# A recommendation model on one Trainium2 core: seven of 416 row gathers are fetched by SP, one row per DMA

## The reference

```python
x = dense_inputs                                   # 2048 x 13
for W, b, g, be in bot:                            # 13 -> 512 -> 256 -> 64
    x = _bn(relu(x @ W + b), g, be)
embs = tbl[idx] for each of 26 tables              # 2048 x 26 x 64, tables 12500 x 64
T = concatenate([embs, x[:, None, :]], axis=1)     # 2048 x 27 x 64
Z = einsum('bnd,bmd->bnm', T, T)
R = concatenate([x, Z[:, upper triangle]], axis=1)
h = R
for W, b, g, be in top:                            # 415 -> 512 -> 256 -> 1
    h = _bn(relu(h @ W + b), g, be)
return sigmoid(h)
```

## Time and profile before

| | |
|---|---|
| median of 3 runs | 581.65 us (581.29 to 582.29) |
| the profiled execution's own time | 581.63 us |
| its span, first to last instruction | 579.8 us |
| busy: PE / DVE / ACT / POOL | 373.9 / 239.1 / 189.4 / 395.8 us |
| gathers of POOL in the loop | 390, mean 946 ns |
| gathers of POOL in the last part | 26, mean 946 ns |
| mean granted clock of PE | 0.763 of full speed |

### The profile page before, as it was taken

How to read it: one execution, slowest core, us unless ns; L and a number is a source line. 1 busy time by engine, 2 the same in 40 slices (tenths; PEclk the granted TensorE clock), 3 DMA queues, 4 the chain that set the end, 5 groups by cost and what they waited for, 6 DMA issues and landing times.

```text
span 579.8 us, 13905 instructions
## 1 busy us (share of the span) xinstructions
PE 373.9 (64%) x5827; PEld 276.7 (48%) x5827; DVE 239.1 (41%) x646; ACT 189.4 (33%) x509; POOL 395.8 (68%) x426
## 2 busy tenths in 40 slices
PE   6959769668778182745638282735638292767995
PEld 2328437466476171533626162533526171556782
DVE  5772254644644242424323242524224142455532
ACT  4742135425325050413214041413214050454223
POOL 5777777777777777777777777777777777771100
PEclk9999787798798577575858566675958566688998
DMA  8222121221212121122122121212212121220000
GB/s 236 61 27 27 26 28 28 29 29 28 30 28 28 27 29 29 28 28 28 26 28 29 28 29 26 29 25 29 29 27 29 26 29 26 29 29 9 2 0 2
DMA packets 15896, 18.31 MB, mean 32 GB/s; under 512 B 7614, under 2 KB 8894, under 8 KB 15695
## 3 DMA queue, kind: packets, MB, share of 16 engines
q0 software_dynamic: 13312, 13.66, 17.7%
q1 hardware_dynamic: 2524, 3.72, 2.0%
HBM read 17.34 MB, written 0.01 MB: 30 GB/s over the span
## 4 chain that ended last, share of the span: by engine, by line
POOL 66%; issue 22%; PE 7%; ACT 1%; DVE 1%; DMA 1%; POOLq 0%; DVEq 0%; ACTq 0%
POOL emb L322 63%; POOL emb L333 3%; PE l_bank L395 3%; PE l_bank L509 1%; PE l_bank L401 1%; ACT Zs L282 1%; PE z_bank L353 1%; DMA emb<-table,stage 0%; PE l_bank L556 0%; DMA idx_raw<-idx 0%; PE l_bank L506 0%; PE tr_bank L481 0%; PE l_bank L518 0%; PE tr_bank L353 0%; ACT logit_sq L696 0%
## 5 line engine op out<-in xcount | busy, mean ns | idle before, releaser
L322 POOL DMA_INDIRECT emb<-table,stage x390 | 368.9, 946 | 121.7 <-issue 118.6
L282 ACT ACTIVATE Zs<-z_bank 27x112 f32<-27x112 f32 (+3 forms) x272 | 92.2, 339 | 210.2 <-PE z_bank L457 204.4
L443 PE MATMUL tr_bank<-ident,emb 128*128 128x128 f32 x195 | 39.5, 328 | 139.4 <-DMA emb<-table,stage 119.5
L256 DVE COPY Zs<-z_bank 27x112 f32<-27x112 f32 (+3 forms) x272 | 88.7, 326 | 48.2 <-PE z_bank L457 43.0
L471 PE MATMUL l_bank<-Zs,tw_sb 128*128 128x128 f32 x840 | 105.8, 279 | 0.0
L471 PEld LDWEIGHTS l_bank<-Zs,tw_sb 128*128 128x128 f32 x840 | 101.3, 196 | 0.0
L855 DVE COPY TT<-tr_bank 128x512 f32<-128x512 f32 (+1 forms) x60 | 55.4, 972 | 108.9 <-PE tr_bank L443 108.3
L443 PEld LDWEIGHTS tr_bank<-ident,emb 128*128 128x128 f32 x195 | 25.3, 160 | 152.2 <-issue 104.5
L457 PE MATMUL z_bank<-TT 64*27 64x26 f32 x3840 | 59.7, 217 | 31.7 <-issue 20.3
L457 PEld LDWEIGHTS z_bank<-TT 64*27 64x27 f32 x3840 | 53.6, 133 | 40.0 <-issue 37.7
L866 DVE BATCH_NORM_STATS2 stats_t<-h_part 128x128 f32 x60 | 17.7, 294 | 110.4 <-ACT hidden_hi L650 110.4
(11 more groups left out here) (124 smaller groups left out, 279.4 us busy)
## 6 DMA issues: line engine op xcount, KB each, us to landing
emb<-table,stage POOLq DMA_INDIRECT x416, 2.7
tw_sb<-tw0x SPq DMA_DIRECT2D x1, 1792.0 KB, 9.2
bw_sb<-bw SPq DMA_DIRECT2D x1, 512.0 KB, 3.7
tw_sb<-tw SPq DMA_DIRECT2D x1, 512.0 KB, 11.9
twx_sb<-twx SPq DMA_DIRECT2D x1, 256.0 KB, 10.0
idx_raw<-idx SPq DMA_DIRECT2D x1, 169.0 KB, 3.1
bw_sb<-bw SPq DMA_DIRECT2D x2, 64.0 KB, 3.8
hidden<-dense_t SPq DMA_DIRECT2D x1, 104.0 KB
```

The source lines that it names most:

```text
L256: last = copy(dst, src[:, :, ZC * q:ZC * q + w])
L282: return nc.scalar.activation(dst, src, ACT.Copy)
L322: pool.indirect_dma_start(out=emb[:, s, k, h, :], out_offset=None, in_=table, in_offset=bass.IndirectOffsetOnAxis(ap=stage[:, s, col:col + ...
L443: tr = nc.tensor.transpose(tr_bank[g % 2][:, c * P:(c + 1) * P], emb[:, s, k, :, :].rearrange("p h d -> p (h d)"), ident[:, :])
```

## The change

SP fetches seven gathers' rows, each row with a DMA of its own: 128 rows of 256 bytes each, 896 DMAs in all. Five of the seven are the gather of pair 12, h = 0, in the third part of each loop iteration (parts 2, 5, 8, 11 and 14, all in slot 2); their rows go straight to their place in `emb`. Two are the gathers of pairs 0 and 1, h = 0, of the last part; their rows go to a new buffer `emb_sp`, which has no other writer, so these rows need no open slot. POOL leaves the seven gathers out.

The row numbers come from a new input `sp_idx`, which SP loads and DVE turns into `sp_rows` with four small operations. SP reads 16 of them at a time into registers, and issues a DMA from each. Before the rows of a part it waits for the slot to be open. The table `SP_ORDER` puts the work in order. PE waits for a semaphore of SP's rows beside that of POOL's.

```diff
+SP_SLOT = SLOTS - 1
+SP_PAIR = TP - 1
+SP_LAST = 2
+SP_SETS = LOOPS + SP_LAST
+SP_BATCH = 16
+SP_ORDER = (("part", 0, 0, 128),
+            ("last", 0, 0, 96),
+            ("part", 1, 0, 128),
+            ("last", 0, 96, 128),
+            ("part", 2, 0, 128),
+            ("last", 1, 0, 64),
+            ("part", 3, 0, 128),
+            ("last", 1, 64, 128),
+            ("part", 4, 0, 128))
...
             sp.dma_start(dense_sb[:, :], dense_t).then_inc(bottom_loaded, 16)
+            sp.dma_start(sp_raw[:, :, :], sp_idx).then_inc(sp_idx_loaded, 16)
             sp.dma_start(bw0_sb[:, :], bw0).then_inc(bottom_loaded, 16)
...
+            regs = [sp.alloc_register("sp_row%d" % r) for r in range(SP_BATCH)]
+            sp.wait_ge(sp_rows_ready, 1)
+            for kind, n, p0, p1 in SP_ORDER:
+                if kind == "part":
+                    sp.wait_ge(slot_open, n * SLOTS + SP_SLOT + 1)
+                for at in range(p0, p1, SP_BATCH):
+                    row_set = n if kind == "part" else LOOPS + n
+                    sp.load(regs, sp_rows[row_set:row_set + 1, at:at + SP_BATCH])
+                    for p, reg in enumerate(regs, at):
+                        row = sp.snap(reg, min_val=0, max_val=NF * VOCAB - 1)
+                        if kind == "part":
+                            sp.dma_start(emb[p:p + 1, SP_SLOT, SP_PAIR, 0, :],
+                                         table[bass.ds(row, 1), :]).then_inc(landed_sp_part, 16)
+                        else:
+                            sp.dma_start(emb_sp[p:p + 1, n, :],
+                                         table[bass.ds(row, 1), :]).then_inc(landed_sp_last[n], 16)
...
                     for k in range(TP):
                         for h in range(2):
+                            if (s, k, h) == (SP_SLOT, SP_PAIR, 0):
+                                continue
...
                     for k in range(k0, k1):
+                        if h == 0 and k < SP_LAST:
+                            continue
...
-                        pe.wait_ge(landed[s][g], (it + 1) * (len(pairs) * 2 * 16))
+                        by_sp = 1 if s == SP_SLOT and SP_PAIR in pairs else 0
+                        pe.wait_ge(landed[s][g], (it + 1) * ((len(pairs) * 2 - by_sp) * 16))
+                        if by_sp:
+                            pe.wait_ge(landed_sp_part, (it + 1) * (P * 16))
...
-                pe.wait_ge(landed_last[h][g], (LAST_GROUPS[g][1] - LAST_GROUPS[g][0]) * 16)
+                k0, k1 = LAST_GROUPS[g]
+                by_sp = SP_LAST if (h, g) == (0, 0) else 0
+                pe.wait_ge(landed_last[h][g], (k1 - k0 - by_sp) * 16)
+                for k in range(by_sp):
+                    pe.wait_ge(landed_sp_last[k], P * 16)
...
+            dve.wait_ge(sp_idx_loaded, 16)
+            step = chain(sp_step, 0)
+            step(nc.vector.tensor_scalar(sp_neg[:, :], sp_raw[:, 0, :], 0.0, float(VOCAB), ALU.is_lt, ALU.mult))
+            step(nc.vector.tensor_tensor(sp_neg[:, :], sp_raw[:, 0, :], sp_neg[:, :], ALU.add))
+            step(nc.vector.tensor_scalar(sp_clamped[:, :], sp_neg[:, :], 0.0, float(VOCAB - 1), ALU.max, ALU.min))
+            nc.vector.tensor_tensor(sp_rows[:, :], sp_clamped[:, :], sp_raw[:, 1, :], ALU.add).then_inc(sp_rows_ready, 1)
             nc.vector.memset(idle_operand[:, :], 0.0).then_inc(consts_ready, 1)
```

More of the change, by code:

```diff
@@ L92, in quadrant_columns, with rec_program @@
     return min(ZC, NF - ZC * q)
-def rec_program(nc, idx, table, dense_t, params, identity, bw0, bw1, bw2, tw0x, twx, tw1, out):
+def rec_program(nc, idx, sp_idx, table, dense_t, params, identity, bw0, bw1, bw2, tw0x, twx, tw1, out):
     ctx = ExitStack()
@@ L114, in rec_program @@
         stage = sb("stage", [P, SLOTS, PW], U32)
+        sp_raw = sb("sp_raw", [SP_SETS, 2, P], I32)
+        sp_neg = sb("sp_neg", [SP_SETS, P])
+        sp_clamped = sb("sp_clamped", [SP_SETS, P])
+        sp_rows = sb("sp_rows", [SP_SETS, P], U32)
+        emb_sp = sb("emb_sp", [P, SP_LAST, D])
         emb = sb("emb", [P, SLOTS, TP, 2, D])
@@ L186, in rec_program @@
         landed = [[sem("landed%d_%d" % (s, g)) for g in range(GROUPS)] for s in range(SLOTS)]
+        sp_idx_loaded = sem("sp_idx_loaded")
+        sp_step = sem("sp_step")
+        sp_rows_ready = sem("sp_rows_ready")
+        landed_sp_part = sem("landed_sp_part")
+        landed_sp_last = [sem("landed_sp_last%d" % k) for k in range(SP_LAST)]
         landed_last = [[sem("landed_last%d_%d" % (h, g)) for g in range(len(LAST_GROUPS))] for h in range(2)]
@@ L476, in last_transposes @@
             def last_transposes(h, g):
-                pe.wait_ge(landed_last[h][g], (LAST_GROUPS[g][1] - LAST_GROUPS[g][0]) * 16)
+                k0, k1 = LAST_GROUPS[g]
[3 more added lines that the diff above has]
+                    pe.wait_ge(landed_sp_last[k], P * 16)
                 for c, (k, k_end) in enumerate(last_blocks(g)):
+                    source = emb_sp if h == 0 and k < SP_LAST else emb_last[:, h, :, :]
                     tr = nc.tensor.transpose(last_tr_bank[g][0:(k_end - k) * D, c * P:(c + 1) * P],
-                                             emb_last[:, h, k:k_end, :].rearrange("p k d -> p (k d)"),
+                                             source[:, k:k_end, :].rearrange("p k d -> p (k d)"),
                                              ident[:, :])
@@ L991 @@
         tw0x[QUAD * q + n, c] = w0[D + row]
+    cols = idx.reshape(UNIT * 2, PARTS, TP, 2)
+    sets = ([(it * SLOTS + SP_SLOT, SP_PAIR) for it in range(LOOPS)] + [(LAST, k) for k in range(SP_LAST)])
+    sp_idx = np.stack([np.stack([cols[:, part, k, 0], (2 * k + np.arange(P) // UNIT) * VOCAB]) for part, k in sets])
     arrays = {
         "idx": np.ascontiguousarray(idx),
+        "sp_idx": np.ascontiguousarray(sp_idx.astype(np.int32)),
         "table": get("L0_rec_emb_tables").reshape(NF * VOCAB, D),
```

## The result

| | before | after |
|---|---|---|
| median of 6 runs | 581.63 us (581.10 to 582.29) | 574.10 us (572.58 to 577.06) |
| ratio | | 0.988, 95% interval 0.9864 to 0.9896 |
| profiled execution, its span | 581.63, 579.8 us | 573.65, 571.8 us |
| gathers of POOL | 416 | 409 |
| rows fetched by SP | 0 | 896 |

What follows compares the result with a forecast made beforehand. The prediction took POOL's gather queue, then the tail, as the bound: 8.75 us off the queue, 1.05 lost in the tail, 7.7 off the 579.8 span, 572.1, plus 1.83 gives 573.9 us; forecast's own range 572 to 577.5, 8-in-10 range 572 to 600.

Steps and rivals of the forecast that it cites:

- POOL's queue: POOL's 416 gathers at 1.25 us each; seven less were to take 8.75 us off.
- The tail: Steps from part 14's last gathers on; the layer needing both halves was to start 7.7 us earlier, waiting for ACT's copies.
- The sum: Whole kernel: span 579.8 - 7.7 = 572.1, with 1.83 us around it 573.9 us.
- SP's part: SP's 896 rows: start at 8.0, one wait for a slot, last row issued at 466.9, 18.5 us before due.
- The cost of a row: On SP: DMA issue 0.31, gap 0.04, address step 0.07, register load 0.085; sum 0.505 us, ends 0.35 and 0.89.
- the limit: Most that a row on SP may cost before SP's rows come late: 0.533 us.
- DVE's idle time: At the start, DVE's 2.73 us idle were to absorb 1.0 and 0.4 us added, so the bottom layers would not be late.
- The due time: SP's rows for pair 12 of part 14: landed by 487.4, issued by about 485.4, taking 2.0 us to land.
- Rival one: SP becomes the bound if a row costs more than 0.533 us; 624.6 us at 0.59 a row; chance 0.30.
- the formula: Span when SP is the bound, c being a row's cost: 8.0 + 896c + 2.0 + 84.2; crosses the old span at 0.542.
- Rival two: SP's DMAs slow POOL's gathers, step 1.25 to 1.27, giving back 8.2 us: about 581.5 us; chance 0.08.

Runs made afterwards that it cites:

- e5_batch4: The change with SP loading 4 row numbers at a time instead of 16; 615.15 us, a single run.
- e7_eight: The change with an eighth gather given to SP, pair 2, h = 0, of the last part, behind its other rows; 603.22 us, ratio 1.039.
- e1_no_rows: The change without SP's loop: neither POOL nor SP fetches the seven gathers, their places hold zeros; 574.10 us, ratio 0.9863.
- e10_batch32: The change with SP loading 32 row numbers at a time instead of 16; 574.83 us, ratio 0.9874.
- e11_pair8_noidle: The change with pair 8 instead of pair 12 and without two idle matmuls before the second half's layer; 574.29 us, ratio 0.9863.
- e13_again: The change once more, unedited, as the measure for other kernels on the same chip; 575.00 us, ratio 0.9873.

## Why the prediction was right

**POOL's queue.** "Seven gathers less are 7 x 1.25 = 8.75 us less of POOL's queue" held: the last gather starts at 514.52 instead of 523.44, 8.9 earlier (forecast 514.7).

**The tail.** Worked out, and then found in the change: PE's transposes 486.27 and 487.57 (486.19, 487.55), products 489.12 (488.89), ACT's copies done 514.02 (513.96), the layer 514.17 (514.45); the last part's first transposes, 510.87 in the earlier trace rows, come at 505.21, 5.66 earlier. All within 0.3 us. One place was wrong: I had the second half's gather landed at 511.2 with 1 us of idle time before it; PE idled 2.07 us and took it up at 512.55. It had started at 508.28, so it was 4.3 us on its way instead of 2.7. So the gather and not the copy bound the layer, by 0.3 us. Why this gather is late I can't say. From its start to PE the same gather took 2.8 us in the kernel before, and 2.85 to 3.25 in the three others whose POOL keeps more than 409 gathers. With all seven gone from POOL it took between 3.0 and 4.3 in the eight kernels where PE waited for it, and 4.0 of these in the one without any of SP's rows.

The sum gave 573.9 and the median is 574.10, but that close a match is partly luck too: the layer gained 7.4 and not 7.7 us, and the change's runs spread over 4.5 us.

**SP's part.** Its first load of row numbers came at 7.2 and its first row at 8.65 (8.0), it waited once for a slot, of part 5 (as said), and had the last row out at 467.7 (466.9). The cost of a row, 0.505 us, was right to the third digit, but that is luck: its terms were not. The issue was 0.225 and not 0.31, the address step 0.044 and not 0.07, the load 0.077 and not 0.085, and I had missed a register move (0.029) and two of three gaps (0.043 each). Two errors of 0.11 to 0.12 us stood against each other. Since 0.533 was the limit, the forecast hung on that sum. Of the rule that I weighed against it, "Runtime: NRT & Kernel Launch" in the Trainium skill, section "Instruction fetch mechanics" (200 ns per register for a load from memory), the runs say that it does not hold for numbers on chip: 56 ns per register and 0.33 us for the load.

One step failed at no cost. I had DVE's idle time take up what the change adds at the start, so that the bottom layers would not be late. They were, by 1.2 us at their end, and the way led past DVE: PE's first matmul waits for the load of `par`, which SP now issues 0.34 us later and for which PE waited 0.66 us longer. POOL, the bound, did not feel it; but the slot of part 5 opened later, at 128.05 instead of 126.87, and SP's first row into it went out at 129.5 to 129.6 instead of 127.5. That takes the most that a row may cost from 0.533 to about 0.530 us, (485.4 - 129.5) / 672.

**The due time.** The limit of 0.533 us for a row agrees with the runs: at 0.53 (batches of 8) nothing was lost, at 0.582 (batches of 4) it was 33.7 us slower than the kernel before on the same chip (581.4). No run lies between the two. Of its terms, PE had the last row 1.1 to 1.2 us behind its issue, where I had taken 2.0.

**The rivals.** Rival one did not come to pass, but it is the right picture of what lies beyond the edge: the formula was off by 2.4 us for a row of 0.582 us. Rival two is excluded, down to 0.6 us, by the two kernels that take the rows away and add them.

## What to carry to other kernels

When one engine's queue is the bound and another is idle, small pieces of work can go to the idle one at a price per piece that looks absurd (here 896 DMAs for seven gathers, 65 us of SP for 1.25 us of POOL), as long as the whole is in before it is due: first work out the due time and the limit per piece, then add up every instruction of a piece, its gaps too. Beyond that limit there is no gentle slope, since each hundredth of a microsecond counts 896 times; keep a margin, as batches of 16 do (the last row was out 18 us before it was due) and those of 8 do not. And read the tail step by step to see what each piece gives there: 8.75 us off the queue were 7.4 at the layer behind it.

## What the runs showed of the hardware

A row DMA from SP (256 bytes, its address in a register) took 0.225 us to issue, less than any DMA of SP in the earlier trace rows (0.31 to 0.61). Where PE waited for the last row, it went on 1.06 us (`e5_batch4`) and 1.21 us (`e7_eight`) after the row's issue had ended. Loads of n row numbers from `sp_rows`, a buffer on the chip, into registers took 0.33 + 0.056n us, for n from 4 to 32.

What spreads the runs of the change over 4.5 us is partly the granted clock in the tail. The same 33 matmuls of the first layer took 2.82 us before, 2.26 in the change and 3.42 without the rows. The windows of that layer, busy time by engine, then the granted clock, for the kernel before:

```profile
521.80:524.60 2.80, 2.80 (x33) 2.73 (x34) 2.54 (x7) 0.50 (x1) 1.97 (x3) 0.61 0.12 25
```

for the change:

```profile
514.40:516.70 2.30, 2.30 (x33) 2.25 (x34) 2.27 (x7) 0.77 (x1) 0.94 (x1) 0.77 0.20 27
```

and for `e1_no_rows`:

```profile
514.20:517.60 3.40, 3.40 (x33) 3.36 (x34) 2.36 (x7) 0.72 (x1) 1.01 (x2) 0.50 0.16 24
```

So the change's profiled execution was lucky by 0.56 us against that of before in this layer, unlucky by as much in the next, that of the second half (3.36 us against 2.80), and lucky by as much again in the matmuls right behind that (1.08 us against 1.64 from line 561 to 573 and from 506 to 518, at a granted clock of 0.91 against 0.61). In sum this is the 0.6 us by which the span gained more than the layer's start. Differences of that size between two single executions of this kernel mean nothing. The second source is POOL: the gathers' median was 947 ns instead of 944 in the traces of `e5_batch4`, `e10_batch32`, `e11_pair8_noidle` and `e13_again`, and 409 times 3 ns are 1.2 us. Both are seen in single executions; why the change's six times spread over 4.5 us and those of before over 1.2, they don't settle. (In the 23 runs of the kernel before that stand beside `e1_no_rows` the spread is 2.3 us.)
